# Three slot attentions: two heads above one another in the rows of the TensorE array

## Chip, cores, metric

The program runs on one NeuronCore of one Trainium2 chip. The time of a kernel is device microseconds (us) of one execution; three executions of the kernel before are at hand, and one execution was taken by the hardware profiler. PE is TensorE's matmul, PEld its weight load, DVE is VectorE, ACT ScalarE, POOL GpSimd, SP the engine that issues most transfers.

## What is computed

A stack of four layers over x (2 batches of 512 rows of 256), each an attention and a feed-forward part. The change touches the slot attentions: 16 heads of 16 features, in layer 1 against a context of 1024 keys with sparsemax, in layer 2's feed-forward part against its own 512 rows with softmax, in layer 3 against 1024 keys with softmax:

```python
q = input @ Wq.T + bq;  k = memory @ Wk.T + bk;  v = memory @ Wv.T + bv
q = _split(q) * HEAD_DIM ** -0.5;  k = _split(k)          # (b, 16 heads, n, 16)
logit = jnp.einsum('bhnd,bhmd->bhnm', q, k)
attn = jax.nn.softmax(logit, axis=-1)                     # layer 1: sparsemax(logit)
out = jnp.einsum('bhnm,bhmd->bhnd', attn, v)
```

## The kernel before, in words

Each layer part is a block with its own instruction stream for every engine; between blocks all engines meet. The names carry the layer: l1 (sparsemax, 1024 keys), m2 (512 keys), l3 (1024 keys). A slot attention is four blocks: normalize, `project_heads` (p), the attention itself (a), `project_out` (o). `HeadTiles` (h) holds the operands of the attention across p and a.

**Operands.** A head has 16 features. A score must be close to float32 but is multiplied as F32R, which runs one pass; so q and k are split into a high and a low part. Of a head, array rows 0 to 63 hold four products of parts (q high twice and q low twice against k high and low in turn), loaded by two DMAs for `qa` and two for `ka` for each group of four heads (`load_qk`, L664 and L667). Rows 64 and 65 hold minus the shift of the softmax (the row's maximum, or sparsemax's threshold), high and low part, against ones in `ka`; rows 66 to 127 are zero in `qa` and one in `ka`, filled by GpSimd (`fill`, L658, L659). So every product has 128 rows. There are three buffers, 8 groups of four heads (4 groups for each batch).

**Dense attention (m2, l3).** A *first product* (L893, 128 queries by 512 keys) goes to PSUM, two at a time as a pair in two banks (two such pairs of banks); VectorE takes the row maximum (L976), in m2 over 512 keys for two rows of results, in l3 over 1024 for one. When all 16 rows of a group are there, TensorE turns them (`turn`, L900), VectorE cuts them into high and low part (`cut`, L985, L987) and SP places them in `qa` with two DMAs (`place`, L853). A *second product* (L909, 128 keys by 512 queries) has the shift in it, ScalarE takes the exponential out of one of three banks (L1037), and the *value products* (L919, float32, four heads in 32 columns each, sent as eight matmuls) sum it with the values. TensorE's order for step t of a group (8 steps in l3, 4 in m2) is: pair, second product of heads 0 and 1, pair, heads 2 and 3, value products of step t-1. The pairs run a group and four pairs ahead. The load of group n+3 is issued when the value products of group n are done.

**Sparse attention (l1).** 16 units of 256 queries and four heads. First products (L1158) go one bank at a time to VectorE, which takes the 8 largest of each 128 (L1263) and from them a first threshold; the same products are made *again* (L1168) for ScalarE, which sums what lies above the threshold (L1435, then twice L1449 from SBUF). After a check (`turn`: L1200, L1202; VectorE reads a flag into a register, L1337 to L1364) the shift is placed (L1120), and second products (L1179, 256 queries), ScalarE's Relu (L1457) and value products (L1191) follow. TensorE works on three units at once, in an order written out in the code.

```python
for h in range(S):                                     # l1, second(u, t)
    ins = nc.tensor.matmul(ps[:, PAIR + 2 * (place % 2) + h // 2, h % 2 * HALF:h % 2 * HALF + HALF],
                           ka[:, buf, h, t * P:(t + 1) * P], qa[:, buf, h, own], start=True, stop=True)
```

## Time and profile before

| | |
|---|---|
| time, three runs | median 3542.73 us (3534.68 to 3547.43) |
| profiled execution | span 3539.1 us from first to last instruction; no time of its own beside that is listed |
| mean granted TensorE clock | 0.839 of 2.4 GHz |
| busy | PE 73%, PEld 46%, DVE 61%, ACT 40%, POOL 11% of the span |
| l1 attention | first products from 852.6, last value products at 1614.9 us |
| m2 attention | first products from 2537.1, last value products at 2682.3 us |
| l3 attention | first products from 3051.5, last value products at 3287.1 us |

The three attentions are about 1143 us of the span. Matmuls are pipelined and their ends are modelled, so that PE "busy" is not PE at its peak.

### The profile page before, as it was taken

Reading aid. Unit: us, or ns where it says so; the run is one execution under the profiler, and the core shown is the slowest. Engines: PE = TensorE matmul, PEld = TensorE weight load, DVE = VectorE, ACT = ScalarE, POOL = GpSimd, SP = SyncE. Lnnn points to the kernel's source line nnn. Section 1 sums busy time; section 2 is a strip of 40 time slices with the busy share of each in tenths; the row PEclk is TensorE's granted clock in tenths of the full one; section 3 lists DMA queues with packets and bytes.
Section 4 is the critical chain, followed back from the end, with each engine's and each line's share of the span. In section 5 each row is a group of like instructions: output and inputs, shape, how many; then the busy total and the mean of one; then the engine's idle time right before and its main releaser. Section 6 shows DMA issues by size and latency. Waiting matters only on the chain. (4 is left out here: it accounts for less than half of the span.)

```text
span 3539.1 us, 37799 instructions
## 1 busy us (share of the span) xinstructions
PE 2583.4 (73%) x12066; PEld 1640.7 (46%) x12066; DVE 2169.0 (61%) x4926; ACT 1432.2 (40%) x2245; POOL 375.1 (11%) x215
## 2 busy tenths in 40 slices
PE   2999998435566566655688458789685896899598
PEld 1444443323233333324588445556343775454387
DVE  4667666566777777743566526655663555676377
ACT  1444443111778887871333121222251231266221
POOL 0000000002000000000533302102110210200011
PEclk7999999767677777776789878989797897899699
DMA  1000000206011111000544200000430110631010
GB/s 56 14 13 14 10 13 2 83 24 195 1 25 25 25 25 25 7 1 10 177 164 161 93 27 1 0 0 0 124 79 23 42 41 14 184 87 40 28 41 30
DMA packets 72294, 170.09 MB, mean 48 GB/s; under 512 B 10184, under 2 KB 38864, under 8 KB 68688
## 3 DMA queue, kind: packets, MB, share of 16 engines
q1 hardware_dynamic: 70608, 164.11, 15.6%
q0 software_dynamic: 1536, 4.20, 0.4%
q8 instruction: 68, 1.11, 0.1%
q14 instruction: 82, 0.67, 0.1%
HBM read 129.09 MB, written 38.80 MB: 47 GB/s over the span
## 5 line engine op out<-in xcount | busy, mean ns | idle before, releaser
L1449 ACT ACTIVATE l1a_over_s<-l1a_sc_s,l1a_minus_step_s 128x1024 bf16<-128x1024 f32 x256 | 290.0, 1139 | 3.9 <-DVE l1a_minus_step_s L1323 2.7
L1263 DVE MAX8 l1a_cand_s<-ps 128x8 f32<-128x128 f32 x1024 | 213.2, 283 | 71.6 <-PE ps L1158 68.4
L1191 PE MATMUL ps<-l1a_probs_s,l1h_v_s 128*32 128x256 f32 x1024 | 123.9, 572 | 157.3 <-ACT l1a_probs_s L1457 156.2
L1914 PE MATMUL ps<-m1e_x_part_s,m1e_up_part_s 128*128 128x256 f32 x1152 | 170.3, 312 | 44.5 <-issue 42.8
L1435 ACT ACTIVATE l1a_sc_s<-ps,l1a_minus_tau_s 128x1024 f32<-128x1024 f32 x128 | 142.1, 1113 | 138.2 <-DVE l1a_minus_tau_s L1292 53.5
L1914 PEld LDWEIGHTS ps<-m1e_x_part_s,m1e_up_part_s 128*128 128x128 f32 x1152 | 163.1, 220 | 47.5 <-issue 45.4
L976 DVE TENSOR_REDUCE l3a_shift_s<-ps 128x1 f32<-128x1024 f32 x128 | 150.2, 1219 | 51.0 <-PE ps L893 51.0
L538 DVE TENSOR_SCALAR l0a_probs_s<-l0a_probs_s 128x1024 f32<-128x1024 f32 x128 | 88.5, 692 | 150.7 <-ACT l0a_probs_s L605 150.2
L605 ACT ACTIVATE l0a_probs_s<-ps 128x1024 f32<-128x1024 f32 x128 | 131.2, 1025 | 104.6 <-PE ps L455 103.4
L1158 PE MATMUL ps<-l1h_ka_s,l1h_qa_s 128*128 128x512 f32 x256 | 131.7, 557 | 56.6 <-DVE l1a_cand_s L1263 46.1
L1037 ACT ACTIVATE l3a_probs_s<-ps 128x512 f32<-128x512 f32 x256 | 132.8, 602 | 88.8 <-PE ps L909 88.5
L1457 ACT ACTIVATE l1a_probs_s<-ps 128x1024 f32<-128x1024 f32 x128 | 125.8, 1016 | 62.1 <-PE ps L1179 62.1
L1179 PEld LDWEIGHTS ps<-l1h_qa_s,l1h_ka_s 128*128 128x128 f32 x512 | 97.3, 264 | 98.7 <-issue 64.8
L1179 PE MATMUL ps<-l1h_qa_s,l1h_ka_s 128*128 128x256 f32 x512 | 129.1, 391 | 17.1 <-ACT l1a_sc_s L1435 12.9
L466 PE MATMUL ps<-l0a_probs_s,l0a_v_s 128*64 128x512 f32 x512 | 138.0, 617 | 0.3 <-ACT l0a_den_s L613 0.3
L469 PE MATMUL ps<-l0a_probs_s,ones 128*64 128x512 f32 x512 | 131.6, 592 | 0.0
L2093 POOL TENSOR_TENSOR m1e_up_part_s<-m1e_up_s,m1e_up_part_s 128x1536 fp32r<-128x1536 f32 x32 | 112.0, 3502 | 161.2 <-ACT m1e_up_part_s L1948 161.1
L455 PE MATMUL ps<-l0a_q_hi_s,l0a_k_parts_s 128*128 128x512 f32 x256 | 122.8, 480 | 2.5 <-PE ps L439 0.3
L1168 PE MATMUL ps<-l1h_ka_s,l1h_qa_s 128*128 128x512 f32 x256 | 98.8, 495 | 30.0 <-ACT l1a_sc_s L1435 30.0
L1191 PEld LDWEIGHTS ps<-l1a_probs_s,l1h_v_s 128*32 128x32 f32 x1024 | 24.7, 134 | 204.8 <-ACT l1a_probs_s L1457 179.6
L1700 PE MATMUL ps<-m3e_x_part_s,m3e_up_part_s 128*128 128x512 f32 x432 | 102.5, 398 | 21.9 <-DVE m3e_x_part_s L1762 18.2
L2555 PE MATMUL ps<-g_qu_part_s,g_k 128*128 128x512 f32 x288 | 98.7, 484 | 26.7 <-DVE g_qu_part_s L2669 26.3
(572 smaller groups left out, 5710.0 us busy)
## 6 DMA issues: line engine op xcount, KB each, us to landing
m1e_up_s<-m_up SPq DMA_DIRECT2D x32, 768.0 KB, 4.3
m1e_down_s<-m_down SPq DMA_DIRECT2D x16, 768.0 KB
l1h_ka_s<-l_k_parts SPq DMA_DIRECT2D x16, 512.0 KB, 7.9
l3h_ka_s<-l_k_parts SPq DMA_DIRECT2D x16, 512.0 KB, 7.9
l0a_w_s<-l_w SPq DMA_DIRECT2D x16, 384.0 KB, 3.0
m3ew_up_s<-m_up SPq DMA_DIRECT2D x6, 768.0 KB, 4.2
m_sorted<-ones SPq DMA_DIRECT2D x1, 4096.0 KB, 16.5
l1h_qa_s<-l_q_parts SPq DMA_DIRECT2D x16, 256.0 KB, 6.0
```

What stands on the lines that cost most here:

```text
L466: nc.tensor.matmul(ps[64 * h:64 * h + 64, 6, :], v[:, p, t, 64 * h:64 * h + 64], probs[:, t % SLOTS, h * NQ:(h + 1) * NQ], start=(t == 0), ...
L469: ins = nc.tensor.matmul(ps[64 * h:64 * h + 64, 7, :], ones[:, 0:64], probs[:, t % SLOTS, h * NQ:(h + 1) * NQ], start=(t == 0), stop=(t == ...
L605: nc.scalar.activation(probs[:, t % SLOTS, :], ps[:, 2 * (t % 2):2 * (t % 2) + 2, :].rearrange("p a n -> p (a n)"), ACT.Exp).then_inc(exp_ ...
L976: nc.vector.reduce_max(shift[:, n % 2, rows * k:rows * k + rows], ps[:, 2 * (at % 2):2 * (at % 2) + 2, :].rearrange("p (r j) n -> p r (j n ...
L1037: nc.scalar.activation(probs[:, t % 2 * S + h, :], ps[:, 4 + i % 3, :], ACT.Exp).then_inc(exp_done, 1)
L1158: nc.tensor.matmul(ps[:, A0 + f % 2, :], qa[:, buf, h, at:at + P], ka[:, buf, h, j * BANK:(j + 1) * BANK], start=True, stop=True).then_inc ...
L1179: ins = nc.tensor.matmul(ps[:, PAIR + 2 * (place % 2) + h // 2, h % 2 * HALF:h % 2 * HALF + HALF], ka[:, buf, h, t * P:(t + 1) * P], qa[:, ...
L1191: ins = nc.tensor.matmul(ps[32 * h:32 * h + 32, VALUES, 0:HALF], v[:, n % 2, t, h, :], probs[:, t % 4, h * HALF:(h + 1) * HALF], start=(t ...
L1263: ins = nc.vector.max(cand[:, r, 8 * (c + j * 4):8 * (c + j * 4) + 8], ps[:, A0 + f % 2, c * P:(c + 1) * P])
L1435: nc.scalar.activation(sc[:, r, :], ps[:, PAIR + 2 * (place % 2):PAIR + 2 * (place % 2) + 2, :].rearrange("p a n -> p (a n)"), ACT.Relu, b ...
L1449: nc.scalar.activation(over[:, done % 2, :], sc[:, r, :], ACT.Relu, bias=minus_step[:, r:r + 1], accum_out=total[:, i, r:r + 1]).then_inc( ...
L1914: ins = nc.tensor.matmul(ps[:, u % 4, way * TOK:(way + 1) * TOK], up_parts[a][:, b % 2, k, way, c, :], x_parts[p][:, b % 2, k, :], start=( ...
```

## The change

**Rows.** Two of the four heads of a group now stand in array rows 0 to 63 and two in rows 64 to 127, each with 48 rows for a first product (q high against k high and k low, q low against k high; the product of the two low parts is left out) and 50 for a second one. `qa` and `ka` hold two slots of heads in place of four. `load_qk` issues eight DMAs for a group where it issued four. GpSimd fills only rows 32 to 63 and 96 to 127 of `ka` with ones, for all three buffers in `project_heads`, where it waited for the last low part before and filled two buffers in the attention. The clearing of rows 64 and 65 for each new group (`shift_cleared`) and the waits on it are gone.

**Order.** A pair is now one product of either half; in the dense attentions the second products go in the order of heads 0, 2, 1, 3, in the sparse one too, and its first products alternate between the halves; `again` keeps both products of a row in one half. VectorE's maximum gives one value for each half, and in l3 the two values of a row (512 keys each) are joined by one small instruction for a group (`join`), for which the turn waits.

```diff
@@ class HeadTiles
-    BUFS, LOADS = 3, 16 * 4
+    BUFS, LOADS = 3, 16 * 8
+    PRODUCT, SHIFTED = 48, 50
+    ORDER = (0, 2, 1, 3)
...
-        self.qa = s.sb("qa", [P, self.BUFS, 4, NQ], F32R)
-        self.ka = s.sb("ka", [P, self.BUFS, 4, nk], F32R)
+        self.qa = s.sb("qa", [P, self.BUFS, 2, NQ], F32R)
+        self.ka = s.sb("ka", [P, self.BUFS, 2, nk], F32R)
...
     def fill(self, pool, buf):
-        pool.memset(self.qa[64:128, buf, :, :].bitcast(F32), 0.0).then_inc(self.filled, 1)
-        pool.memset(self.ka[64:128, buf, :, :].bitcast(F32), 1.0).then_inc(self.filled, 1)
+        for half in range(2):
+            pool.memset(self.ka[64 * half + 32:64 * half + 64, buf, :, :].bitcast(F32), 1.0).then_inc(self.filled, 1)
+        pool.wait_ge(self.filled, 2 * buf + 2)
+    def rows(self, h, count):
+        return slice(64 * (h // 2), 64 * (h // 2) + count)
     def load_qk(self, sp, n):
...
+        if n < self.BUFS:
+            sp.wait_ge(self.filled, 2 * n + 2)
+        for half in range(2):
+            at, two = 64 * half, slice(2 * half, 2 * half + 2)
+            q_hi, q_lo = (self.q_parts[part, n:n + 1, :, two, :].rearrange("o r h n -> (o r) (h n)") for part in range(2))
+            sp.dma_start(self.qa[at:at + 32, buf, :, :].rearrange("r h n -> r (h n)").bitcast(F32),
+                         q_hi.unsqueeze(1).to_broadcast([16, 2, 2 * NQ])).then_inc(self.qk_loaded[buf], 16)
+            sp.dma_start(self.qa[at + 32:at + 48, buf, :, :].rearrange("r h n -> r (h n)").bitcast(F32), q_lo
+                         ).then_inc(self.qk_loaded[buf], 16)
+            sp.dma_start(self.ka[at:at + 32, buf, :, :].rearrange("r h n -> r (h n)").bitcast(F32),
+                         self.k_parts[n:n + 1, :, :, two, :].rearrange("o r a h n -> (o r a) (h n)")
+                         ).then_inc(self.qk_loaded[buf], 16)
+            sp.dma_start(self.ka[at + 32:at + 48, buf, :, :].rearrange("r h n -> r (h n)").bitcast(F32),
+                         self.k_parts[n:n + 1, :, 0:1, two, :].rearrange("o r a h n -> (o r a) (h n)")
                          ).then_inc(self.qk_loaded[buf], 16)
@@ project_heads, gpsimd
-            pool.wait_ge(lo_ready, U)
-            tiles.fill(pool, 0)
-            pool.wait_ge(tiles.filled, 2)
+            for buf in range(tiles.BUFS):
+                tiles.fill(pool, buf)
@@ dense_attention: sync, gpsimd, tensor, vector
-                if n >= BUFS:
-                    sp.wait_ge(shift_cleared, n - BUFS + 1)
...
-            tiles.fill(pool, 1)
-            tiles.fill(pool, 2)
...
-            for n in range(G - BUFS):
-                pool.wait_ge(pv_done, NC_ * (n + 1))
-                pool.memset(qa[64:66, n % BUFS, :, :].bitcast(F32), 0.0).then_inc(shift_cleared, 1)
...
+                r, j = divmod(k, NH)
+                slot, t = divmod(r, QT)
                 for half in range(2):
-                    r, j = divmod(2 * k + half, NH)
-                    h, t = divmod(r, QT)
-                    ins = nc.tensor.matmul(ps[:, 2 * (at % 2) + half, :], qa[:, buf, h, t * P:(t + 1) * P],
-                                           ka[:, buf, h, j * BANK:(j + 1) * BANK], start=True, stop=True)
+                    own = tiles.rows(2 * half, tiles.PRODUCT)
+                    ins = nc.tensor.matmul(ps[:, 2 * (at % 2) + half, :], qa[own, buf, slot, t * P:(t + 1) * P],
+                                           ka[own, buf, slot, j * BANK:(j + 1) * BANK], start=True, stop=True)
...
+                pe.wait_ge(joined, n + 1)
...
-                nc.tensor.matmul(ps[:, 4 + i % 3, :], ka[:, buf, h, t * P:(t + 1) * P], qa[:, buf, h, :],
+                nc.tensor.matmul(ps[:, 4 + i % 3, :], ka[own, buf, h % 2, t * P:(t + 1) * P], qa[own, buf, h % 2, :],
                                  start=True, stop=True).then_inc(scored, 1)
...
+            def join(n):
+                dve.wait_ge(pair_used, pair_place((n + 1) * PAIRS - 1) + 1)
+                if NH == 1:
+                    nc.vector.sem_inc(joined, 1)
+                else:
+                    nc.vector.tensor_tensor(shift[:, n % 2, 0, :], shift[:, n % 2, 0, :], shift[:, n % 2, 1, :], ALU.max
+                                            ).then_inc(joined, 1)
@@ sparse_attention: tensor
+        def scanned(i, half):
+            (tt, slot), j = divmod(i // NH, 2), i % NH
+            return S * tt + 2 * half + slot, j
...
-                for j in range(NH):
-                    f = FIRST * u + NH * r + j
+                for half in range(2):
+                    r, j = scanned(i, half)
+                    buf, h, at = where(u, r)
+                    own = tiles.rows(h, tiles.PRODUCT)
+                    f = FIRST * u + 2 * i + half
...
-                for h in range(S):
+                for h in tiles.ORDER:
+                    own = tiles.rows(h, tiles.SHIFTED)
                     ins = nc.tensor.matmul(ps[:, PAIR + 2 * (place % 2) + h // 2, h % 2 * HALF:h % 2 * HALF + HALF],
-                                           ka[:, buf, h, t * P:(t + 1) * P], qa[:, buf, h, own], start=True, stop=True)
+                                           ka[own, buf, h % 2, t * P:(t + 1) * P], qa[own, buf, h % 2, now],
+                                           start=True, stop=True)
```

## Rows read from the trace of the kernel before

**Rows 1.** The page: the span of the profiled execution
```profile
span 3539.1 us, 37799 instructions
```
**Rows 2.** Windows: us; PE, PEld, DVE, ACT, POOL busy; PEclk, DMA share, GB/s
```profile
927.00:1592.00 665.00, 408.09 (x1942) 210.27 (x1942) 454.63 (x1877) 530.04 (x854) 9.00 (x5) 0.74 0.07 18
1592.00:1612.00 20.00, 18.31 (x82) 9.42 (x82) 4.13 (x6) 6.89 (x7) 0.00 (x0) 0.50 0.01 2
...
3042.00:3050.00 8.00, 0.00 (x0) 0.00 (x0) 0.00 (x0) 0.00 (x0) 0.00 (x0) 0.70 1.05 409
3051.00:3078.00 27.00, 23.26 (x41) 10.44 (x41) 22.96 (x22) 1.28 (x1) 10.92 (x5) 0.50 0.69 156
3079.00:3245.00 166.00, 166.00 (x853) 84.64 (x851) 128.23 (x121) 114.53 (x220) 9.01 (x5) 1.00 0.29 68
```
**Rows 3.** Timeline, one step of l3: start us, us, engine, line, idle before
```profile
3143.07 0.74 PE L893 MATMUL ps<-l3h_ka_s,l3h_qa_s 128*128 128x512 f32 x2
...
3143.66 0.63 PE L909 MATMUL ps<-l3h_qa_s,l3h_ka_s 128*128 128x512 f32 x2
3143.86 2.36 DVE L976 TENSOR_REDUCE l3a_shift_s<-ps 128x1 f32<-128x1024 f32 x2 [0.74 <-PE ps L893]
...
3144.09 2.06 ACT L1037 ACTIVATE l3a_probs_s<-ps 128x512 f32<-128x512 f32 x4 [1.03 <-PE ps L909]
...
3144.58 0.66 PE L909 MATMUL ps<-l3h_qa_s,l3h_ka_s 128*128 128x512 f32 x2
3144.74 0.19 PEld L909 LDWEIGHTS ps<-l3h_qa_s,l3h_ka_s 128*128 128x128 f32 x1 [0.19 <-ACT l3a_probs_s L1037]
3145.17 1.06 PE L919 MATMUL ps<-l3a_probs_s,l3h_v_s 128*32 128x512 f32 x8
3146.17 0.30 PEld L893 LDWEIGHTS ps<-l3h_ka_s,l3h_qa_s 128*128 128x128 f32 x2 [0.84 <-issue]
```
**Rows 4.** Timeline of m2: a load of group, and TensorE's wait for it
```profile
2567.57 0.57 SPq L664 DMA_DIRECT2D m2h_qa_s<-m_q_parts  x1
...
2569.42 0.58 SPq L667 DMA_DIRECT2D m2h_ka_s<-m_k_parts  x1
...
2574.94 0.73 PE L893 MATMUL ps<-m2h_ka_s,m2h_qa_s 128*128 128x512 f32 x2 [2.13 <-DMA m2h_ka_s<-m_k_parts]
```
**Rows 5.** Transfers of l3, 3028 to 3300: KB each, us from issue to landing
```profile
l3h_ka_s<-l_k_parts SPq DMA_DIRECT2D x16, 512.0 KB, 7.9
l3h_qa_s<-l_q_parts SPq DMA_DIRECT2D x16, 256.0 KB, 6.1
```
**Rows 6.** Transfers of m2, 2520 to 2700
```profile
m2h_ka_s<-m_k_parts SPq DMA_DIRECT2D x16, 256.0 KB, 5.3
...
m2h_qa_s<-m2a_minus_lo_s SPq DMA_DIRECT2D x8, 8.0 KB, 1.8
```
**Rows 7.** Waits in m2, 2554 to 2650: us in total, times, longest
```profile
PE ps L893 <- DMA m2h_ka_s<-m_k_parts: 11.2, 5, 2.5
```
**Rows 8.** Timeline: pairs of m2 while nothing but VectorE is fed
```profile
2540.87 2.35 DVE L976 TENSOR_REDUCE m2a_shift_s<-ps 128x2 f32<-128x1024 f32 x2 [0.18 <-PE ps L893]
...
2543.41 2.36 DVE L976 TENSOR_REDUCE m2a_shift_s<-ps 128x2 f32<-128x1024 f32 x2 [0.18 <-PE ps L893]
```
**Rows 9.** Timeline: m2 at the lower clock
```profile
2591.66 1.05 PE L909 MATMUL ps<-m2h_qa_s,m2h_ka_s 128*128 128x512 f32 x2
...
2592.86 1.93 PE L919 MATMUL ps<-m2a_probs_s,m2h_v_s 128*32 128x512 f32 x8
...
2594.72 0.72 PE L893 MATMUL ps<-m2h_ka_s,m2h_qa_s 128*128 128x512 f32 x2
```
**Rows 10.** Timeline: end of a unit of l1, and the turn of the unit before
```profile
1101.37 0.28 DVE L1336 TENSOR_REDUCE l1a_worst_all_s<-ps 1x1 f32<-1x128 f32 x1 [1.77 <-PE ps L1200]
...
1139.15 1.22 PE L1179 MATMUL ps<-l1h_qa_s,l1h_ka_s 128*128 128x256 f32 x4
...
1144.36 1.20 PE L1168 MATMUL ps<-l1h_ka_s,l1h_qa_s 128*128 128x512 f32 x4
```

More of the change, by code:

```diff
@@ L830, in dense_attention @@
         qk_loaded, v_loaded = tiles.qk_loaded, tiles.v_loaded
-        shift = s.sb("shift", [P, 2, ROWS])
+        shift = s.sb("shift", [P, 2, NH, ROWS])
+        joined = s.sem("joined")
         minus_hi, minus_lo = s.sb("minus_hi", [ROWS, P], F32R), s.sb("minus_lo", [ROWS, P], F32R)
@@ L899, in turn, with second @@
                 pe.wait_ge(pair_used, max(at - 1, pair_place((n + 1) * PAIRS - 1) + 1))
-                nc.tensor.transpose(ps[0:ROWS, 2 * (at % 2), 0:P], shift[:, n % 2, :], ident[:, :]
+                pe.wait_ge(joined, n + 1)
+                nc.tensor.transpose(ps[0:ROWS, 2 * (at % 2), 0:P], shift[:, n % 2, 0, :], ident[:, :]
                                     ).then_inc(shift_turned, 1)
-            def second(n, t, h):
-                i, buf = (n * NC_ + t) * S + h, n % BUFS
-                if t == 0 and h == 0:
+            def second(n, t, q):
+                i, buf, h = (n * NC_ + t) * S + q, n % BUFS, tiles.ORDER[q]
+                own = tiles.rows(h, tiles.SHIFTED)
+                if t == 0 and q == 0:
                     pe.wait_ge(shift_placed, 32 * n + 32)
@@ L917, in value_products @@
                     pe.wait_ge(o_copied, n)
-                for h in range(S):
+                for q, h in enumerate(tiles.ORDER):
                     ins = nc.tensor.matmul(ps[32 * h:32 * h + 32, VALUES, :], v[:, n % 2, t, h, :],
-                                           probs[:, t % 2 * S + h, :], start=(t == 0), stop=(t == NC_ - 1))
+                                           probs[:, t % 2 * S + q, :], start=(t == 0), stop=(t == NC_ - 1))
                 ins.then_inc(pv_done, 1)
@@ L950, in _ @@
                 for t in range(NC_):
-                    for h in range(S):
-                        i = EARLY + 2 * (n * NC_ + t) + h // 2
-                        if h % 2 == 0 and i < ALL:
+                    for q in range(S):
+                        i = EARLY + 2 * (n * NC_ + t) + q // 2
+                        if q % 2 == 0 and i < ALL:
                             first_pair(i)
-                        second(n, t, h)
+                        second(n, t, q)
                     if t == TURN_AT and n < G - 1:
@@ L1020, in _ @@
                     cut(n)
+                if i % PAIRS == PAIRS - 1:
+                    join(i // PAIRS)
             cut(G - 1)
@@ L1164, in again @@
                 place = again_place(u, r)
+                own = tiles.rows(h, tiles.PRODUCT)
                 if place >= 2:
@@ L1177, in second @@
                 pe.wait_ge(pair_used, place - 1)
-                for h in range(S):
+                for h in tiles.ORDER:
+                    own = tiles.rows(h, tiles.SHIFTED)
                     ins = nc.tensor.matmul(ps[:, PAIR + 2 * (place % 2) + h // 2, h % 2 * HALF:h % 2 * HALF + HALF],
-                                           ka[:, buf, h, t * P:(t + 1) * P], qa[:, buf, h, own], start=True, stop=True)
+                                           ka[own, buf, h % 2, t * P:(t + 1) * P], qa[own, buf, h % 2, now],
+                                           start=True, stop=True)
                 ins.then_inc(pair_made, 1)
@@ L1221, in spread_bank @@
                                  start=True, stop=True).then_inc(spread_made, 1)
-            for r in range(ROWS):
-                first_row(0, r)
+            for i in range(ROWS):
+                first_rows(0, i)
             for u in range(UNITS + 1):
@@ L1255, in wide, with candidates @@
                 return a.unsqueeze(2).to_broadcast([P, ROWS, m])
-            def candidates(u, r):
-                for j in range(NH):
-                    f = FIRST * u + NH * r + j
+            def candidates(u, i):
+                for half in range(2):
+                    r, j = scanned(i, half)
+                    f = FIRST * u + 2 * i + half
                     dve.wait_ge(rows_made, f + 1)
```

62 lines of the change are left out of this document (21 added, 41 removed).

## The prediction

> **What bounds the kernel now.** I read the page first, for the span of 3539.1 us [rows 1], then the stages by windows, because a share over the whole span says little of three attentions that run one after another, and then the timeline of one step in each. In l3 the reader is to see that from 3079 to 3245 us TensorE is busy for all of the 166 us at the full 2.4 GHz, VectorE for 128.23 and ScalarE for 114.53 [rows 2]: TensorE's order is the bound there, and a step of it can be laid out in links [rows 3]. The step begins with the first pair at 3143.07 and ends where the next begins at 3146.17, 3.10 us later. Its links: pair to second products, 0.59 (to 3143.66); from there to the fourth second product, whose weight load begins at 3144.74, 0.19 us late because it waits for ScalarE to empty its bank; that product, the last of the two that span 3144.58 to 3145.24, starts one product (0.40) earlier, at 3144.84: 1.18. Then 0.33 to the value products at 3145.17, and 1.00 for these. VectorE's two maxima take 2.36 of the 3.10, ScalarE's four exponentials 2.06.
>
> In m2 the steps are alike, but TensorE also waits for the load of the next group, 11.2 us in five places [rows 7]; there, load and first use lie 7.37 us apart (2567.57 to 2574.94) [rows 4]. In l1 ScalarE is busy for 530.04 of 665 us, VectorE for 454.63, TensorE for 408.09, at a mean clock of 0.74 [rows 2]: ScalarE is near its limit, and TensorE matters only where ScalarE waits for it.
>
> **The dense step after the change.** All products stay in number and in columns. What can shrink is the time of two products that stand in different halves. No row of before has two row tiles at work; the nearest is the value products: eight matmuls in 1.00 us, in four column strips, where two F32R products one behind the other start 0.23 apart (0.63 for two, 0.40 for one), so that eight in a row would take at least 1.84 [rows 3]. Strips of columns do run beside one another here, and I take it that halves of rows do so too. Then the pair costs what its first product costs. In the pair at 3143.07 the second product starts 0.34 after the first (0.74 for two, less 0.40), the first weight load not being hidden. So the second products start 0.34 after the pair in place of 0.59. The next link does not shrink: the fourth second product needs the bank that the exponential of the first one empties, and that chain (product 0.40, exponential 0.6, weight load) is the same. Nor do the last two. Step: 0.34 + 1.18 + 0.33 + 1.00 = 2.85, a gain of 0.25. VectorE's 2.36 stays under it. Bounds: 0 if halves run one after another; at most 3.10 - 2.36 = 0.74, where VectorE ends it.
>
> The Trainium skill bears on this: TensorEngine Tiling (Array Packing), Theoretical Speedup, gives a factor of up to two where the contraction has at most 64 rows. The eight products of a step would fall from 8 x 0.23 to 4 x 0.23, 0.92 less; by it the step would be 2.36, VectorE's, and not 2.85. I go by the wait for ScalarE in the row.
>
> **l3:** 64 steps x 0.25 = 16.0 less. Ahead of them 20 pairs feed only VectorE, at the lower clock (0.50) [rows 2]; in m2's like, VectorE takes 2.36 for two of them and then waits 0.18 for TensorE, 2.54 from start to start (2540.87 to 2543.41) [rows 8]. Side by side a pair is shorter by more than that wait, so I take the 0.09 of each pair away: 20 x 0.09 = 1.8. The join (0.17 by its like, 0.3 with its waits, eight times) lies in VectorE's idle 0.74 of a step; if that cover were gone it would cost 2.4.
>
> **Loads.** For a group of l3 before: 2 x 512 + 2 x 256 = 1536 KB [rows 5]; now 48 rows for each head in place of 64, 1152 KB, in m2 768 for 1024 [rows 6]. The first load stands in the queue ahead of the stores of v, for which the next block waits with all engines idle at 409 GB/s (3042 to 3050) [rows 2]. A load moves 1024 KB in 7.37 us, of which 1.8 is what even a small transfer takes [rows 4, 6]: 184 KB a us. 384 KB fewer are 2.1 us sooner for l1 and l3 each, 256 KB 1.4 for m2: 5.6 at most, nothing if the stores are late for another reason; I take 4.6, the queue being full. SP has four more issues of 0.6 us for each load [rows 4]. What is queued behind them is v and the placing of the next shift, which comes a turn later in the group, at least two steps: covered; uncovered, 2.4 us late in each group. In m2 the last issue comes not 1.85 but 7 x 0.61 = 4.3 us after the first. A small transfer lands 1.8 after its issue, one behind others 5.3 [rows 6]; I take 2.7, since each of the eight is done about when the next is issued: 7.0 for 7.37, bounds 6.1 and 9.6. That is 5 x 0.4 = 2.0 less, between 6.5 less and 11 more.
>
> **m2:** of 32 steps, ten stand ahead of such a wait, where a gain only lengthens it; 22 x 0.25 = 5.5, plus 2.0, plus 12 leading pairs x 0.09 = 1.1.
>
> **The clock.** While the three stretches of pairs alone ran, 23.26 of 27 us busy, the clock stayed at 1.2 GHz; at the end of l1 it did so through 18.31 of 20 us [rows 2]. It was up in l3 from 3079 on, when second products had joined the pairs. With halves beside one another TensorE does the same in less time, so I expect it to rise later, or to fall oftener behind m2's waits. At the lower clock the value products take 1.86 to the next pair (2592.86 to 2594.72), and two products 1.05 for 0.63 [rows 3, 9]; the links that hold a product grow by 0.2 to 0.4. A step then is 0.5 + 1.6 + 0.55 + 1.86 = 4.5, 1.65 more than 2.85. I put two such steps into m2 and one and a half into l3: 3.3 and 2.5 back. The fills now run beside VectorE's copies of the projection: unseen in before, from 0 to 2 us each; 0.5 each, 1.5.
>
> **l1.** VectorE's and ScalarE's instructions are the same. At the end of a unit ScalarE waits for TensorE, at the lower clock: four second products take 1.22 [rows 10]; two by two they save two starts of 0.21, for two groups 0.86. Behind the value products follow four products that are made again (1.20, at the full clock), all in one half, and then the turn; VectorE waits 1.77 for it, so what TensorE saves there counts, up to 1.77. If these four run at 1.2 GHz they take 2.1 and the saving is gone. Half of one and half of the other, 0.4 to 0.5, for 16 units: 8, between 21 less (0.86 and as much as 0.45 more from first products beside repeated ones) and 8 more (0.5 each, if the repeated ones lose the full clock and nothing is saved before). The first unit's 16 pairs, like the dense ones, give 16 x 0.09 = 1.5.
>
> **Sum:** l3 16.0 + 1.8 - 2.5 = 15.3; m2 5.5 + 2.0 + 1.1 - 3.3 = 5.3; l1 9.5; loads ahead of the blocks 4.6; fills -1.5: 33.2 less. The profiled execution has a span of 3539.1, 3.6 below the median of 3542.7 and inside the spread of its runs; 3505.9 plus 3.6 gives 3510.
>
> **The rivals.** (a) *The clock does not rise.* Through a whole l3 and m2 at 1.2 GHz, 96 steps of 4.5 in place of 3.10 are 134 more, less the 16 that do not depend on it: about 3660. For it: the stretches at 0.50 with TensorE nearly always busy. Against: once at 2.4 GHz, l3 kept it to the end. It decides from 20 slow steps on (33 / 1.65), a fifth of them; with 30 the time is 3560. The Trainium skill, TensorE: Matmul & The Clock Gate, The HAM clock gate, says that the lower clock is the default and activity lifts it; the rows agree, 0.50 behind idle and 1.00 in l3's steps. (b) *The halves do not run beside one another*, so the change doesn't do what it says: only the loads' 4.6 + 2.0 less 1.5 stay, 3538. For it: no row shows row tiles. (c) *VectorE ends the step*: 2.36 in place of 3.10, 96 x 0.74 = 71, less 5 that m2's waits take, plus 21 of l1 and 7 of the rest: 3449. Against it stands the fourth product's wait in every step. It is what the Trainium skill's factor of two, cited above, would lead to. (d) *The eight loads of m2 land late*, 9.6: 11 + 2 back, 3523, still faster.
>
> **How the numbers follow.** Forecast with (d) 0.60; (a) in its full or partial form 0.17; (b) 0.13; (c) 0.05; 0.05 for something else in l1, either way. One measurement can tell 0.3%, 10.6 us, from no change. Faster: forecast, (c) and half the rest, less the edge of the forecast that loses in l1: 0.67. Same: (b) and that edge, 0.15. Slower 0.18. The bounds of l1 (21 less, 8 more), of the loads and of the step (0 to 0.74, likeliest 0.15 to 0.35) make the forecast's own range 3480 to 3532; for eight in ten it reaches down to 3475 and up into the partial form of (a), 3565.
>
> **What would show it.** A step of l3 at 2.85, with the two products of a pair starting together and the load of the fourth second product still waiting for ScalarE; the granted clock of l3's steps at 1.00; landing to first use in m2 near 7.0 us after the first issue; the blocks p ending 1 to 2 us sooner. Wrong it would be made by granted clocks of 0.50 in l3's steps, pairs that still take 0.74, or a unit of l1 (44.3 us, 665 us in 15) that grows.

## The result, and the profile after

The kernel after takes 3579.32 us (median of four, 3578.05 to 3585.59), the kernel before 3539.34 (3534.68 to 3547.43): ratio 1.012, interval 1.0101 to 1.0138, so slower by 1.2%. The forecast was 3510; the time lies above the wider range of the prediction too (3475 to 3565). The profiled execution has a span of 3578.8 us and a mean granted clock of 0.774 (0.839 before).

**The steps are as forecast.** First one step of l3 at 2.4 GHz, by the timeline; it answers to [rows 3].

```profile
3191.44 0.18 PEld L899 LDWEIGHTS ps<-l3h_ka_s,l3h_qa_s 48*128 48x128 f32 x2 [0.84 <-issue]
3191.44 0.50 PE L899 MATMUL ps<-l3h_ka_s,l3h_qa_s 48*128 48x512 f32 x2
...
3191.78 0.40 PE L917 MATMUL ps<-l3h_qa_s,l3h_ka_s 50*128 50x512 f32 x2
...
3192.21 2.07 ACT L1056 ACTIVATE l3a_probs_s<-ps 128x512 f32<-128x512 f32 x4 [0.77 <-PE ps L917]
...
3192.86 0.18 PEld L917 LDWEIGHTS ps<-l3h_qa_s,l3h_ka_s 50*128 50x128 f32 x1 [0.65 <-ACT l3a_probs_s L1056]
...
3193.29 1.06 PE L927 MATMUL ps<-l3a_probs_s,l3h_v_s 128*32 128x512 f32 x8
3194.28 0.50 PE L899 MATMUL ps<-l3h_ka_s,l3h_qa_s 48*128 48x512 f32 x2
```

Both products of the pair, in either half, fill 0.50 us where they filled 0.74; the second products start 0.34 after the pair; the fourth one's weight load still waits for ScalarE, now 0.65 instead of 0.19; start to start is 2.84 us. A step of the same kernel at 1.2 GHz:

```profile
3219.00 0.79 PE L899 MATMUL ps<-l3h_ka_s,l3h_qa_s 48*128 48x512 f32 x2
...
3221.62 1.94 PE L927 MATMUL ps<-l3a_probs_s,l3h_v_s 128*32 128x512 f32 x8
3223.49 0.79 PE L899 MATMUL ps<-l3h_ka_s,l3h_qa_s 48*128 48x512 f32 x2
```

4.49 us, 1.65 more. How many steps are of this kind is what went wrong. Windows of after, columns as in [rows 2]:

```profile
3070.00:3078.00 8.00, 0.00 (x0) 0.00 (x0) 0.00 (x0) 0.00 (x0) 0.00 (x0) 0.76 1.01 392
3079.00:3103.00 24.00, 15.99 (x43) 5.94 (x43) 22.84 (x23) 1.12 (x1) 0.35 (x1) 0.50 0.72 143
3103.00:3277.00 174.00, 166.43 (x853) 63.91 (x851) 129.10 (x126) 112.91 (x219) 0.00 (x0) 0.83 0.25 53
3277.00:3324.00 47.00, 40.18 (x143) 11.45 (x140) 11.05 (x14) 22.02 (x43) 0.00 (x0) 0.70 0.00 1
2561.00:2667.00 106.00, 97.56 (x400) 36.68 (x400) 61.21 (x64) 55.00 (x107) 0.00 (x0) 0.64 0.20 54
927.00:1592.00 665.00, 430.06 (x1902) 190.40 (x1902) 456.97 (x1876) 522.72 (x841) 0.00 (x0) 0.52 0.07 15
```

Of before, the windows of l3's last steps and of m2's steps:

```profile
3244.00:3285.00 41.00, 36.14 (x144) 12.10 (x142) 11.08 (x13) 21.69 (x43) 0.00 (x0) 0.88 0.00 1
2554.00:2650.00 96.00, 84.82 (x403) 42.80 (x402) 62.27 (x64) 56.37 (x107) 9.01 (x5) 0.93 0.32 73
```

The steps of l3 that have pairs (3103 to 3277) were granted 0.83 on the mean where they had 1.00 [rows 2], though TensorE is busy for 166.43 of 174 us; the last steps, without pairs, 0.70 for 0.88; m2's 0.64 for 0.93; l1 0.52 for 0.74 [rows 2].

In the table an attention goes from its first product to its last matmul, which spreads the reciprocals of the sums and ends 8 to 10 us behind the last value product. The parts of l3 are cut at the first second product, at the last pair and at the last value product, so they leave these 8 to 10 us out. The "tail" is what follows the last pair: ten steps in l3 and six in m2 that have no pairs. "At 1.2" is the time in which the granted clock is the lower one.

| us | before | after |
|---|---|---|
| l1: start of p to first product / attention (at 1.2) | 45.3 / 771.0 (440) | 48.9 / 778.9 (752) |
| m2: the same | 29.7 / 154.4 (42) | 29.4 / 171.3 (127) |
| l3: the same | 46.4 / 244.7 (40) | 50.0 / 259.4 (126) |
| l3 attention in parts: leading pairs / steps with pairs / tail | 27.6 / 165.3 / 43.3 | 24.5 / 173.3 / 51.4 |

The three attentions are 39.5 longer, the blocks ahead of them 6.9, and parts that the change does not touch happened to be 6.7 shorter: 39.7, the difference of the spans.

**l1.** Groups of ScalarE's instructions over the whole attention; behind the second bar stands what it waited for. Before, then after:

```profile
L1435 ACT ACTIVATE l1a_sc_s<-ps,l1a_minus_tau_s 128x1024 f32<-128x1024 f32 x128 | 142.1, 1113 | 138.2 <-DVE l1a_minus_tau_s L1292 53.5 <-DVE l1a_shift_s L1364 40.8 <-PE ps L1168 34.2
L1457 ACT ACTIVATE l1a_probs_s<-ps 128x1024 f32<-128x1024 f32 x128 | 125.8, 1016 | 62.1 <-PE ps L1179 62.1
```

```profile
L1455 ACT ACTIVATE l1a_sc_s<-ps,l1a_minus_tau_s 128x1024 f32<-128x1024 f32 x128 | 142.1, 1112 | 158.3 <-DVE l1a_minus_tau_s L1312 54.7 <-DVE l1a_shift_s L1384 51.9 <-PE ps L1185 41.0
L1477 ACT ACTIVATE l1a_probs_s<-ps 128x1024 f32<-128x1024 f32 x128 | 126.5, 1018 | 46.2 <-PE ps L1197 46.2
```

The second products side by side save ScalarE 15.9 us of waiting (62.1 to 46.2). Its waits ahead of L1435, for VectorE's thresholds and check and for the products made again, grow by 20.1 (138.2 to 158.3), of which 11.1 are the check's and 6.8 those products'; TensorE is now at 1.2 GHz nearly throughout (752 of 778.9 us). A third wait, for the last value products of a unit, grows by 4.6, before and after:

```profile
L1463 ACT ACTIVATE l_o_all<-ps 128x256 f32<-128x256 f32 x16 | 6.2, 385 | 14.3 <-PE ps L1191 14.3
L1483 ACT ACTIVATE l_o_all<-ps 128x256 f32<-128x256 f32 x16 | 6.1, 384 | 18.9 <-PE ps L1210 18.9
```

With 0.9 less at L1449 (3.9 to 3.0) the waits add up to the 7.9 by which the attention is longer. It is the trade that the prediction named, with the wrong sign of the sum.

**The blocks p.** VectorE's groups in l1's projection, after and then before:

```profile
L793 DVE CAST l1p_hi_s<-l1p_full_s 128x512 fp32r<-128x512 f32 x12 | 11.4, 951 | 1.8 <-DMA l_k_parts<-l1p_lo_s 0.8 <-ACT l1p_full_s L781 0.8 <-DMA l_q_parts<-l1p_lo_s 0.3
L795 DVE TENSOR_TENSOR l1p_lo_s<-l1p_full_s,l1p_hi_s 128x512 fp32r<-128x512 f32 x12 | 8.3, 692 | 0.4
```

```profile
L778 DVE CAST l1p_hi_s<-l1p_full_s 128x512 fp32r<-128x512 f32 x12 | 5.1, 426 | 3.1 <-ACT l1p_full_s L766 1.6 <-DMA l_k_parts<-l1p_lo_s 1.3 <-DMA l_q_parts<-l1p_lo_s 0.2
```

Beside GpSimd's fills a copy takes 951 ns on the mean of twelve, for 426; the subtraction behind it keeps its 692. (The Trainium skill, SBUF — State Buffer, Who interferes with whom, says that copies and casts of VectorE can need a port that it shares with GpSimd, one blocking the other, and that an operation of two inputs meets only GpSimd's reads: the trace agrees, these fills only write.)

**m2's load**, three lines of the timeline, answering to [rows 4]: from the first issue over the last one to the first use.

```profile
2578.03 0.61 SPq L675 DMA_DIRECT2D m2h_qa_s<-m_q_parts  x1
...
2581.95 0.42 SPq L682 DMA_DIRECT2D m2h_ka_s<-m_k_parts  x1
...
2584.85 0.50 PE L899 MATMUL ps<-m2h_ka_s,m2h_qa_s 48*128 48x512 f32 x2 [1.60 <-DMA m2h_ka_s<-m_k_parts]
```

6.82 us, for 7.0 forecast and 7.37 before.

### The profile page after: what moved, and what is told of

Its sections match the earlier page's. It is cut to its first block and busy times, and to the rows that moved or that the text cites. A ratio compares the mean times of both kernels' runs of the same rounds, so it can differ in the third digit from the quotient of the medians.

```text
span 3578.8 us, 37893 instructions
## 1 busy us (share of the span) xinstructions
PE 2619.4 (73%) x12065; PEld 1579.1 (44%) x12066; DVE 2194.5 (61%) x4934; ACT 1431.3 (40%) x2245; POOL 336.1 (9%) x200
## 5 line engine op out<-in xcount | busy, mean ns | idle before, releaser
L1210 PE MATMUL ps<-l1a_probs_s,l1h_v_s 128*32 128x256 f32 x1024 | 137.0, 628 | 160.8 <-ACT l1a_probs_s L1477 159.0
L1455 ACT ACTIVATE l1a_sc_s<-ps,l1a_minus_tau_s 128x1024 f32<-128x1024 f32 x128 | 142.1, 1112 | 158.3 <-DVE l1a_minus_tau_s L1312 54.7
L1174 PE MATMUL ps<-l1h_ka_s,l1h_qa_s 48*128 48x512 f32 x256 | 166.2, 734 | 43.7 <-DVE l1a_cand_s L1283 33.9
L986 DVE TENSOR_REDUCE l3a_shift_s<-ps 128x2 f32<-128x1024 f32 x128 | 149.6, 1221 | 54.8 <-PE ps L899 54.8
L1934 PEld LDWEIGHTS ps<-m1e_x_part_s,m1e_up_part_s 128*128 128x128 f32 x1152 | 158.8, 214 | 47.7 <-issue 45.5
L1185 PE MATMUL ps<-l1h_ka_s,l1h_qa_s 48*128 48x512 f32 x256 | 135.8, 653 | 29.8 <-ACT l1a_sc_s L1455 29.8
L1477 ACT ACTIVATE l1a_probs_s<-ps 128x1024 f32<-128x1024 f32 x128 | 126.5, 1018 | 46.2 <-PE ps L1197 46.2
L2113 POOL TENSOR_TENSOR m1e_up_part_s<-m1e_up_s,m1e_up_part_s 128x1536 fp32r<-128x1536 f32 x32 | 112.0, 3502 | 158.3 <-ACT m1e_up_part_s L1968 158.2
L1174 PEld LDWEIGHTS ps<-l1h_ka_s,l1h_qa_s 48*128 48x128 f32 x256 | 67.4, 298 | 119.5 <-DVE l1a_cand_s L1283 107.9
L2575 PE MATMUL ps<-g_qu_part_s,g_k 128*128 128x512 f32 x288 | 98.2, 482 | 26.3 <-DVE g_qu_part_s L2689 26.0
L2600 PE MATMUL ps<-g_attn_s,g_v 128*128 128x512 f32 x192 | 94.5, 624 | 25.6 <-DVEq L2736 21.8
```

What stands on the lines that cost most here:

```text
L986: nc.vector.reduce_max(both, ps[:, 2 * (at % 2):2 * (at % 2) + 2, :], AX.X).then_inc(pair_used, 1)
L1174: nc.tensor.matmul(ps[:, A0 + f % 2, :], qa[own, buf, h % 2, at:at + P], ka[own, buf, h % 2, j * BANK:(j + 1) * BANK], start=True, stop=Tr ...
L1185: ins = nc.tensor.matmul(ps[:, PAIR + 2 * (place % 2) + j, :], qa[own, buf, h % 2, at:at + P], ka[own, buf, h % 2, j * BANK:(j + 1) * BANK ...
L1210: ins = nc.tensor.matmul(ps[32 * h:32 * h + 32, VALUES, 0:HALF], v[:, n % 2, t, h, :], probs[:, t % 4, h * HALF:(h + 1) * HALF], start=(t ...
L1455: nc.scalar.activation(sc[:, r, :], ps[:, PAIR + 2 * (place % 2):PAIR + 2 * (place % 2) + 2, :].rearrange("p a n -> p (a n)"), ACT.Relu, b ...
L1934: ins = nc.tensor.matmul(ps[:, u % 4, way * TOK:(way + 1) * TOK], up_parts[a][:, b % 2, k, way, c, :], x_parts[p][:, b % 2, k, :], start=( ...
```

## Experiments

Theory A: how many of the array's rows the products occupy counts for the clock. Theory B: only the time counts in which TensorE is busy, and halves side by side leave it idle. Ratios are against the kernel before, on the same chip. "l3" is in parts as in the table above.

**Which of the two.** All four heads in rows 0 to 63, in the old order:

```
-    ORDER = (0, 2, 1, 3)
+    ORDER = (0, 1, 2, 3)
     def rows(self, h, count):
-        return slice(64 * (h // 2), 64 * (h // 2) + count)
+        return slice(0, count)
...
```

(The cut leaves out that `qa` and `ka` have four slots of heads again, and that the loads and the maximum follow them.)

> The kernel after, but all four heads of a group in rows 0 to 63 (48 for a first product, 50 for a second one) and in the order of the kernel before: every product has its columns and its place, none can run beside another, and half of the array's rows are never used by them. A step of l3 at the full clock should be 3.1 us again. Theory A (rows count for the clock): l1 at 0.50 from start to end (750 us), l3 above 80 and m2 above 100 us at 0.50, time 3590 to 3610. Theory B (only the time counts in which TensorE is busy): 440, 40 and 40 us at 0.50 in l1, m2 and l3 as in the kernel before, time 3540 to 3550.

Ratio 1.055 (1.052 to 1.059); four executions took 3719 to 3779, the profiled one 3738, and the ratio is that of the two shorter ones. At 1.2 GHz: 807 us of l1, 165 of m2, 266 of l3. Windows over l3's steps with pairs and a part of them, and a step at the full clock:

```profile
3183.00:3432.00 249.00, 249.00 (x850) 121.75 (x849) 131.32 (x120) 117.17 (x219) 0.00 (x0) 0.62 0.19 37
3321.00:3447.00 126.00, 126.00 (x370) 58.96 (x369) 52.43 (x48) 51.40 (x96) 0.00 (x0) 0.50 0.14 28
```

```profile
3240.28 0.72 PE L898 MATMUL ps<-l3h_ka_s,l3h_qa_s 48*128 48x512 f32 x2
...
3243.35 0.72 PE L898 MATMUL ps<-l3h_ka_s,l3h_qa_s 48*128 48x512 f32 x2
```

The step is the old one, 3.07 us. TensorE is busy for all of the 249 us, and still the clock falls from 1.00 to 0.50 within them; for 126 us on end it stays there, where the kernel before, as busy, had 1.00 throughout [rows 2]. Theory B alone is out: with 48 and 50 rows in place of 128 in the first and second products and the same columns in the same order (the product of the two low parts is left out, as in the kernel after), the clock does not hold. The time, forecast at 3590 to 3610, was underestimated twice over: there are more slow steps than thought, and one takes 5.6 us by the timeline (3368.86 to 3374.44), for 4.5 side by side. What this run cannot split is the number of rows from the array's being divided in two: both came together.

Two earlier runs had aimed at the same question and mixed it up. One kept both halves but took each pair from one:

> The kernel after with its 48 and 50 rows, but the two products of a pair both in one half, the second products in the order of heads 0, 1, 2, 3, and the first products of l1 in the old order: nearly nothing runs side by side, and TensorE is as long busy as in the kernel before. Theory A: the clock is no better than in the kernel after (l1 all at 0.50, l3 and m2 with long stretches at 0.50), and the steps are longer at that (3.1 at the full clock, about 4.7 at the lower): 3590 to 3620. Theory B: the clock is that of the kernel before (l3 at 1.00 from start to end, mean near 0.84), and only the slower fills stay, about 3548.

Ratio 1.0146 (1.0129 to 1.0163), 3589.6; 746, 128 and 106 us at 1.2 GHz. This is A's side, but many steps took 2.87 us: the pair from one half ran beside second products of the other, so that it was no test of anything one after another. The other took the rows of zeros out of the first products of the kernel before:

```
-  qa[:, buf, h, t * P:(t + 1) * P], ka[:, buf, h, j * BANK:(j + 1) * BANK]
+  qa[0:64, buf, h, t * P:(t + 1) * P], ka[0:64, buf, h, j * BANK:(j + 1) * BANK]
...                                                     # the same in l1's first products and in those made again
```

> The kernel before, with the 64 rows of zeros taken out of its first products alone (rows 0 to 63 of 128; second products keep 128); the output does not change, nothing runs side by side, every product has its columns. Theory A: the clock falls, in l1 above all, where two thirds of the products are first ones (mean 0.74 before, 0.50 to 0.6 then), and the time rises by 5 to 15 us, to about 3550. Theory B: clock 0.84 and time 3539 as before, within 0.3 per cent.

Ratio 1.0252 (1.0228 to 1.0276), 3624: neither theory. l1 is 38 us longer and at 1.2 GHz for 680 us in place of 440, but l3 is 31 longer with the clock up (44 us at 1.2). The timeline of l3 there:

```profile
3188.14 0.73 PE L909 MATMUL ps<-l3h_qa_s,l3h_ka_s 128*128 128x512 f32 x2
...
3188.81 0.29 PEld L893 LDWEIGHTS ps<-l3h_ka_s,l3h_qa_s 64*128 64x128 f32 x2 [0.37 <-issue]
3188.81 0.73 PE L893 MATMUL ps<-l3h_ka_s,l3h_qa_s 64*128 64x512 f32 x2
3189.47 0.30 PEld L909 LDWEIGHTS ps<-l3h_qa_s,l3h_ka_s 128*128 128x128 f32 x2 [0.36 <-ACT l3a_probs_s L1037]
3189.47 0.73 PE L909 MATMUL ps<-l3h_qa_s,l3h_ka_s 128*128 128x512 f32 x2
```

At each change between 64 and 128 rows the weight load stands idle for 0.36 to 0.37 us and starts when the product before is all but through; two products then take 0.66 start to start where those of one kind can take 0.46 (2 x 0.23 [rows 3]), and a step 3.65 by the median. (The Trainium skill, TensorEngine Tiling (Array Packing), Key Properties, says that changing the tiling mode drains TensorE: the trace agrees.) So this run says little of the clock.

**Can the clock be kept up?** Extra products, overwritten by those that follow in the same bank, ahead of the second pair of a step (in the shade of the wait of 0.65) and of the leading pairs:

```
                 r, j = divmod(k, NH)
+                if i < EARLY or i % 2 == 1:
+                    nc.tensor.matmul(ps[:, 2 * (at % 2), :], ka[0:128, buf, 0, 0:P], ka[0:128, buf, 0, 0:BANK], ...)
```

> The kernel after, with one extra product (128 rows, 512 columns, its result overwritten) ahead of the second pair of each dense step and ahead of the leading pairs; the output does not change. At the full clock it lies in the 0.65 us that TensorE waits for ScalarE before the fourth second product. Theory A (the clock goes by how much of the array's rows the products occupy) and theory B (it goes by the time that TensorE is busy, and the halves side by side leave it idle) both expect l3's steps at a granted clock of 1.00 nearly throughout, 2.85 each, and a time 10 to 20 us below the kernel after, about 3563. If neither is right, the extra products only cost: 3579 or more, and the clock as before them.

> The same extra products with 64 rows instead of 128: as many columns, as long in TensorE, half the array's rows. Theory A: the granted clock of m2 and l3 gains less than half of what 128 rows gain, and the time stays within 5 us of the kernel after, 3575 to 3585. Theory B: the same clock and the same time as with 128 rows, about 3563.

> The kernel after, with two extra products of 64 rows, one in either half and so side by side, where the kernel with one extra product of 64 rows has one; TensorE is about as long busy as there. Theory A: the second half's rows raise the clock more: less than 50 us at 0.50 in l3 (76 there) and less than 50 in m2 (74 there), time near 3545. Theory B: the time of the kernel with one extra product of 64 rows, 3552, and its 76 and 74 us.

| | ratio | m2 (at 1.2) | l3 (at 1.2) | l3 in parts |
|---|---|---|---|---|
| after | 1.012 | 171.3 (127) | 259.4 (126) | 24.5 / 173.3 / 51.4 |
| one extra, 128 rows | 1.0058 (1.0041 to 1.0074) | 158.4 (63) | 250.8 (80) | 30.9 / 158.8 / 50.9 |
| one extra, 64 rows | 1.0042 (1.0025 to 1.0059) | 159.2 (74) | 243.4 (76) | 27.2 / 154.8 / 51.2 |
| 64 rows in either half | 1.0028 (1.001 to 1.0045) | 154.5 (62) | 243.9 (73) | 27.2 / 155.7 / 50.7 |

More work in TensorE lifts the clock and takes 0.6 to 0.9% off the kernel after, 22 to 33 us by the ratios. With the products in either half, m2 and l3 are back at 154.5 and 243.9 us, which is what they take in the kernel before (154.4 and 244.7): the whole loss of these two stages has come back. A step at the full clock is no shorter for it (2.84 with the 128 rows, 3150.59 to 3153.43), so it is the clock that gives: that the clock was the loss in m2 and l3 is shown.

How much of l3 runs at 1.2 GHz differs between executions. The kernel after with its fills moved (below) spent 81 us of l3 there without any extra product, and 23 us of its steps with pairs, where this table's first line has 60; in the nine runs with extra products ahead of the second pair of a step these steps have 3 to 13. m2 is steadier, 126 to 131 us in three runs without them and 49 to 74 in the nine with them. So the 126 to 76 of l3 is not to be taken as the worth of one product, and the ratios count.

Theory A's own forecast failed: an extra product of 64 rows did at least as much as one of 128 (3551.6 us, where A had 3575 to 3585 and B 3563). The comparison is not clean, since the one of 128 rows among those of 48 and 50 brings the changes of the run before; the leading pairs take 30.9 for 27.2 with it. A second half on top came out at 3542, A's time, with 73 and 62 us at 1.2 GHz, nearer to B's 76 and 74, and the intervals of the ratios overlap. Of rows alone the clock does not go by these runs; how rows and busy time are weighed stays open. (The Trainium skill, TensorE: Matmul & The Clock Gate, The HAM clock gate, lets activity lift the clock, which these runs show as well, m2's time at 1.2 GHz falling from 127 to 62 us.)

**l1 alone.** With l1 wholly as in the kernel before:

```
-            tiles = HeadTiles(nc, ...)
+            tiles = (WholeRows if sparse else HeadTiles)(nc, ...)    # WholeRows: HeadTiles of before
```

> l1 as in the kernel before (operands, fills, loads, functions), m2 and l3 as in the kernel after; output unchanged. If the change in l1 costs what the stage shows, l1's projection and attention are back at 36.0 and 771 us with a granted clock of 0.74 between, 11.5 less, and the time is 3568. If l1's loss is only the shift of clock from elsewhere (m2 and l3 then lose more), the time stays within 4 us of 3579.

Ratio 1.0108 (1.0089 to 1.0128), 3572.2. l1 is back at 45.9 ahead and 768.3 us (417 at 1.2), m2 and l3 are unchanged at 172.5 and 259.2. The stages show 13.6 less, medians and ratios 4 to 7; the attention of l1 differs by 8 us between traces of kernels in which it is the same (768.3 to 776.1). In the traces with the changed l1 it takes 778.7 to 781.9, longer in each, so that l1's loss is real but known only to some us. And the other way, extra products in l1 (on top of those of the last run of the table):

```
                     pe.wait_ge(pair_used, place - 1)
+                whole = tiles.rows(h, 64)
+                for j in range(NH):
+                    nc.tensor.matmul(ps[:, PAIR + 2 * (place % 2) + j, :], ka[whole, buf, 0, 0:P], ka[whole, buf, 0, 0:BANK], ...)
                 for j in range(NH):
...                                                     # one more of either half ahead of every four second products
```

> The kernel after with the two extra products in m2 and l3, and in l1 two extra products of 64 rows ahead of every row that is made again (in that row's half) and ahead of every four second products (one in either half). If l1 grew because its clock never rises, the clock there reaches 0.7 or more, l1 returns to 771 or below (as forecast, 762), and the time is 8 to 16 us under 3542. If l1 is bound by ScalarE and VectorE and only pays for more work in TensorE's order, the extra products lengthen it: 780 to 800, time 3545 to 3565.

Ratio 1.0223 (1.021 to 1.0236), 3616, far above either forecast; l1 takes 852.0 us, 729 of them still at 1.2 GHz. ScalarE's group there:

```profile
L1468 ACT ACTIVATE l1a_sc_s<-ps,l1a_minus_tau_s 128x1024 f32<-128x1024 f32 x128 | 142.2, 1112 | 215.1 <-PE ps L1194 86.9 <-DVE l1a_shift_s L1397 64.0 <-DVE l1a_minus_tau_s L1325 54.7
```

Its waits grow from 158.3 to 215.1: in l1 a product ahead of those made again is on ScalarE's path, and the clock hardly rises for it (123 us at 2.4 GHz for 27).

**The fills** behind the last low part:

```
+            pool.wait_ge(lo_ready, U)
             for buf in range(tiles.BUFS):
                 tiles.fill(pool, buf)
```

> The kernel after, with GpSimd's fills put back behind VectorE's last low part of the projection, output unchanged. If the fills slow VectorE's copies, the projections of l1, m2 and l3 end 3.8, 1.6 and 4.4 us sooner (copies at 427 ns again), and the time is 7 to 10 us below the kernel after, about 3570. If the copies are slow for another reason (the stores, the order of GpSimd's other work), the time stays at 3579 or, as the first load then waits for the fills, rises.

> The kernel after with the two extra products, and with the fills put back behind the last low part. The same edit without extra products gave 3563 to 3593 in four runs, so that fills and clock could not be told apart. Against the 3542 of the extra products alone: near 3540 if the fills cost what projection and start of the attention together show (0.8 in l1, 1.8 in l3, nothing in m2), near 3533 if they cost the whole 3.0 and 4.0 by which the projections' ends move.

Ratios 1.0131 (1.0098 to 1.0163) and 1.0032 (1.002 to 1.0044), against 1.012 and 1.0028 without the edit: no gain either time. VectorE's copies are back at 426 ns and in the first of the two runs the projections of l1 and l3 end 3.0 and 3.9 us sooner, but the first load now waits for the fills, and from the start of p to the first product l1 and l3 are only 0.9 and 1.8 shorter and m2 1.3 longer.

**What is left of the gain with the clock up.** l1 as before, dense parts with extra products in either half, in four steps:

> l1 as in the kernel before, m2 and l3 as in the kernel after with the two extra products of 64 rows, one in either half, ahead of the second pair of a step and of the leading pairs; output unchanged. If the two remedies add up (l1's 11 and the extra products' 36 under the kernel after's 3579), the time is near 3532, within 0.3 per cent of the kernel before. If l1's part is taken back by later stages, it stays at 3542, that of the extra products alone.

> The same, with the extra products also ahead of the first pair of each step for the first eight steps. If l3's clock rises late (3098 instead of 3079 in the trace of before) because the first steps still lack activity, it rises up to 10 us sooner, l3 is 3 to 5 us shorter, and the time is near 3528. If it rises at the same point, the extra products cost 0.2 to 0.4 for each of eight steps, twice: 2 to 6 us more than without them.

```
+                for half in (0, 1, 0, 1)[:4 if i < EARLY else 2 * (i % 2)]:     # dense_extra_lead2
...
```

> l1 as in the kernel before, m2 and l3 as in the kernel after, with two extra products in either half ahead of each leading pair (one in either half until now) and one in either half ahead of the second pair of a step; output unchanged. If the leading pairs can be made to lift the clock, l3's steps begin at 1.00, 16 slow steps of 4.5 become steps of 2.85, and l3 is up to 20 us shorter: about 3520. If the clock still rises only at 3098 or so, the leading pairs grow (three starts of 0.43 at the lower clock for VectorE's 1.18 of a pair): 20 x 0.1 to 0.3 more, 3540 to 3545.

> The kernel with l1 as before and two extra products in either half ahead of each leading pair, with extra products also in the steps that have no pairs (the last ten of l3 and six of m2): two ahead of the first and of the third second product of a step, two of the upper half behind the spread of the reciprocals; output unchanged. In its parent l3's tail (last pair to last value products) takes 50.7 us at 0.50 for 43.3 in the kernel before, m2's 34.4 for 32.7, while l3's steps with pairs take 154.5 for 165.3. If the clock of the tail is what gives the steps' gain back, l3's tail falls to 43 to 45 and the time to 3528 to 3533, faster than the kernel before by 0.2 to 0.3 per cent. If the tail is bound by the chain of reciprocals and ScalarE, or the extra products hold it up, it stays at 50 or grows, and the time at 3540 or more.

| | us | ratio | m2 | l3 (at 1.2) | l3 in parts |
|---|---|---|---|---|---|
| before | 3537 to 3538 | | 154.4 | 244.7 (40) | 27.6 / 165.3 / 43.3 |
| extra products | 3537.4 | 0.9997 (0.9987 to 1.0008) | 154.6 | 243.8 (73) | 27.3 / 157.2 / 50.8 |
| also in the first eight steps | 3542.8 | 1.0013 (1.0004 to 1.0021) | 155.7 | 242.9 (65) | 27.7 / 155.6 / 51.1 |
| two in either half on leading pairs | 3539.4 | 1.0004 (0.9995 to 1.0013) | 154.3 | 240.0 (42) | 26.3 / 154.5 / 50.7 |
| also in the tail | 3537.5 | 1.0004 (0.9993 to 1.0015) | 156.3 | 238.4 (34) | 27.2 / 154.8 / 48.3 |

Windows of the third, over the parts of l3:

```profile
3051.00:3077.00 26.00, 21.53 (x125) 11.48 (x121) 23.73 (x23) 0.68 (x1) 0.00 (x0) 0.90 0.65 132
3077.00:3231.00 154.00, 153.54 (x956) 64.26 (x956) 128.22 (x126) 113.02 (x218) 0.00 (x0) 0.99 0.28 60
3231.00:3278.00 47.00, 40.42 (x147) 11.54 (x143) 11.36 (x14) 21.85 (x43) 0.00 (x0) 0.71 0.00 1
```

The clock is up through the steps (0.99), and they take 10.8 us less than before: 54 steps of 0.20. The gain of the halves is real where extra products keep the clock up. It is given back in the tail (7.4) and ahead of the attention (3.9), and m2, with 49 us at 1.2 GHz for 42, gains nothing. In the second run the clock rose sooner (65 us at 1.2 GHz for 73), as hoped, but the products cost more than that gave. The last kernel went for the tail; a row of the kernel before there, then three of its own:

```profile
3264.30 1.22 PE L940 MATMUL ps<-l3a_rden_parts_s,spread 64*128 64x512 f32 x2 [3.12 <-DVE l3a_rden_parts_s L1003]
```

```profile
3254.55 1.22 PE L1007 MATMUL ps<-l3a_rden_parts_s,spread 64*128 64x512 f32 x2 [3.12 <-DVE l3a_rden_parts_s L1083]
3255.57 1.06 PE L959 MATMUL ps<-l3h_ka_s 64*128 64x512 f32 x2
...
3256.56 1.94 PE L986 MATMUL ps<-l3a_probs_s,l3h_v_s 128*32 128x512 f32 x8
```

TensorE stands 3.12 us waiting for the reciprocals before the extra products come, the clock has dropped (value products 1.94), and 2.4 of the 7.4 are regained. The kernel before has the same wait of 3.12 and drops too, but is back at the full clock after 10.2 us; the third kernel of the table after 30.7, this one after 17.1. So the wait isn't new: what the halves lose in the tail is the time until the clock rises again. None of the four came down to the time that its expectation hoped for (3532, 3528, 3520, 3528 to 3533). The control, the kernel before with extra products on its leading pairs:

> The kernel before, with two extra products of 128 rows ahead of each leading pair of m2 and l3, output unchanged: the control for what extra products do without the change. If they lift the clock in the leading pairs, m2 and l3 start their steps at 1.00, each up to 3 us sooner, time 3530 to 3537. If not, four starts of 0.43 at the lower clock exceed VectorE's 1.18 of a pair: 20 and 12 leading pairs by 0.5, 16 us more, about 3553.

Ratio 1.0015 (1.0004 to 1.0026), 3543: only 18 us of l3 at 1.2 GHz, but the leading pairs 28.7 for 27.6 and the steps as before. The early clock alone is worth nothing there, and the time came out between the two that were expected. No kernel here beats the kernel before.

## Why the prediction was wrong

Between the 33.2 less of the forecast and the 39.7 more of the spans lie 72.9 us: l3 30.0, m2 22.2, l1 17.4, the blocks ahead of the attentions 10.0, less the 6.7 of parts that are the same.

1. *The step*, 2.85 and 4.5: right, 2.84 and 4.49; so was the wait that stays, the pair's 0.34 and m2's landing (6.82 for 7.0). Rivals (b), (c) and (d) are out. The leading pairs gained more than forecast, 3.1 for 1.8 in l3 and 1.9 for 1.1 in m2.
2. *The clock*, the step that failed: "I put two such steps into m2 and one and a half into l3". In l3 it is 12 of the 54 with pairs: (173.3 - 54 x 2.84) / 1.65. Steps with pairs became 8.0 longer instead of 13.5 shorter. The tail became longer by 8.1 in l3 and 8.5 in m2 (41.2 for 32.7). The prediction multiplied its 0.25 by 64 and counted the ten steps of l3's tail in, though the 0.25 is gained between a pair and the second products behind it and these steps have no pair; and it put no slow step there. In place of 15.3 and 5.3 less, the attentions are 14.7 and 16.9 longer. The reasoning took TensorE's busy time alone: the same work in less time, so a little later and oftener at the lower clock. The run in rows 0 to 63 shows that fewer rows let the clock fall while TensorE is never idle. The warning was in hand as rival (a), in its partial form of 30 slow steps put at 3560, with 0.17 for it and the full form together. That form sized m2 and l3 well: their 52.2 us off are 32 steps of 1.65 beyond the 3.5 foreseen. What lies above 3560 comes from l1 and the blocks ahead.
3. *l1*, 9.5 less: 7.9 more. The prediction's outer bound was 8 more, if the repeated products lose the full clock, and they did: 0.52 for 0.74. That the number fits is luck, since the bound supposed that nothing is saved in front. The gain at the second products came and was sized well, 15.9 / 16 = 1.0 a unit for 0.86; the loss, 20.1 / 16 = 1.3 a unit, was put at 0.9 at most and given half a chance, and the 4.6 behind the value products were not seen. The first pairs of l1, put at 1.5 less, take 0.8 more (85.0 for 84.2).
4. *The loads*, 4.6 less: from VectorE's last instruction of the projection to the first product it is 0.2 less in l1, 0.2 in m2 and 0.9 in l3 (there 9.90 before, 3041.58 to 3051.48, and 9.04 after, 3069.83 to 3078.87). In l1 the last store of v is issued when VectorE has made v; from there to the next block's first load it is 9.07 us before (843.42 to 852.49) and 9.06 after (847.60 to 856.66), so there the queue was not what it waited for. *The fills*, 1.5 more: they lengthen the projections by 3.8 and 4.4 us in l1 and l3 and not at all in m2, beyond the 2 us each that the prediction had as its most; with the fills out of the way only 1.4 of it came back in the first products.

What is shown: the clock as the cause in m2 and l3 (runs with extra products), fewer rows or an array in halves as something that lowers it (rows 0 to 63 alone), l1's trade by ScalarE's waits. Argued from traces only: that l1's 20.1 are the clock's, since l1's clock could not be lifted without new work. Open: how rows and busy time weigh together, whether it is the rows or the division of the array, and why the clock takes three times as long to come back in the tail.

## What to carry to other kernels

Before products are packed into fewer rows so that they run side by side, ask what holds TensorE's clock up in that stage: rows of zeros that look like waste may be part of it, and the step here is 8% shorter than the old one at the full clock (2.84 for 3.10), and at the lower clock 58% longer than itself (4.49). Where a wait is left in TensorE's order, an extra product in it can hold the clock; where there is none, as ahead of l1's repeated products, it costs its time. Such products only bought back here what the change had lost. Don't mix products of 64 and 128 rows in turn: each change costs the weight load's cover.

## What the hardware showed that was not expected

- TensorE busy without a gap for 126 us at 1.2 GHz, with first and second products of 48 and 50 rows; the same order with 128 rows ran at 2.4 GHz for 166 us.
- After the same wait of 3.12 us in l3's tail the clock was back after 10.2 us with products of 128 rows and after 30.7 with halves.
- Changes between products of 64 and 128 rows, four in a step, make it 0.55 us longer (3.65 for 3.10), 31 us in l3.
- VectorE's copy of 128x512 takes 951 ns for 426 beside GpSimd's memset of 32 rows; the subtraction of two inputs from SBUF is not touched.
- One extra product of 64 rows in every step of m2 took its time at 1.2 GHz from 127 to 74 us, one of 128 rows to 63; l3's 126 went to 76 and 80, but a run without any had 81.
